# Two embedding features fetched row by row from SyncE and ScalarE beside GpSimd's gathers, their addresses multiplied once

## The chip, the core and the metric

The kernel runs on one core of a Trainium2 chip. A core has a matrix engine (TensorE, PE in the profile, its weight loads PEld), VectorE (DVE), ScalarE (ACT), GpSimd (POOL), a sequencer that mostly issues transfers (SyncE, SP) and 16 DMA engines. The metric is the device time of one execution in microseconds (us); lower is better.

## The reference

A batch of 2048 samples looks up 27 rows of 128 floats, one in each of 27 tables. The 27 vectors, all their 351 pairwise dot products and 16 dense numbers make a row of 3823, which goes through a small network:

```python
e = stack([tbl_f[ids[:, f]] for f in range(27)], axis=1)      # 2048 x 27 x 128
inter = einsum('bfd,bgd->bfg', e, e)[:, triu_i, triu_j]       # 351 pairs
h = concatenate([e.reshape(2048, -1), inter, dense_ctx], 1)   # 3823
h = maximum(h @ W_top1 + b_top1, 0)                           # 512
h = maximum(h @ W_top2 + b_top2, 0)                           # 256
y = h @ W_top3                                                # 1
```

Tables 22 and 23 have 1000 rows each.

## The kernel before

The batch is cut into 16 tiles of 128 samples, numbered 0 to 15. There is no planner: each engine's program is a loop over the tiles with the order written out by hand, and semaphores tie the engines.

**GpSimd** gathers. For every tile it issues one indirect DMA for each feature (L294), which brings 128 rows of one table into one 128-column stretch of `emb`. `emb` has room for one tile only. The features are in seven groups of up to four (0 to 3, ..., 20 to 23, 24 to 26). Before the gathers of group g of tile t, GpSimd waits until TensorE has turned group g of tile t-1 (L286).

**TensorE** turns each feature (a transpose into PSUM, L323, in `turn_group`), after a wait for all gathers of that group. ACT rounds the result to the matmul's format (`split_group`, L609) and DVE takes the rest (L745), so each feature is multiplied three times (L352 to L354). Within a tile the order is: multiply group 0, turn 2 and 3, multiply, turn 4 and 5 (with the columns of the tile before), multiply and finish the columns, turn 6, then 16 units of pairwise products (L377) between multiplies, and towards their end turn groups 0 and 1 of the next tile. The last matmuls of a tile are layer 2 of the tile before (L470). The last tile has an order of its own with finer steps.

**SyncE** loads the first layer's weights in 30 pieces through six stages (L219); a stage is free when DVE has split it (`s_w_lo`). Behind them come seven small loads of ids (L243), the second layer's weights, the dense inputs and constants. After that SyncE fetches feature 23 of seven tiles (3, 5, ..., 15) one row at a time. It loads 32 ids into registers (L261), and for each row works out the offset and issues a DMA of 512 bytes (L266) into `ahead`, which has a place for each of the seven sets. GpSimd leaves those seven gathers out, so it issues 425 in all. In `turn_group` TensorE waits for all 128 rows of a set before it turns group 5 of that tile (L319).

**ACT** issues no DMA before the change. In tile t it rounds groups 1, 2, 3, places the context columns, rounds 4, takes the columns (`take_columns`), rounds 5 and 6, applies the first ReLU, and then copies units of pairwise products (L665) to the tile's end.

Of the kernel before, what the change touches and what calls it, by code (L numbers as in the profile page):

```python
# [5 lines left out]
def dlrm_tower_kernel(nc, dense_ctx, ids, tables, w_top1, b_top1, w_top2, b_top2, w_top3, out):  # L6
    fp32 = mybir.dt.float32
    fp32r = mybir.dt.float32r
    i32 = mybir.dt.int32
    ALU = mybir.AluOpType  # L10
# [46 lines left out]
    AHEAD_TILES = [3, 5, 7, 9, 11, 13, 15]  # L57
    NA = len(AHEAD_TILES)
    LOAD = 32
    HALF = H1 // 2  # L60

    ctx = ExitStack()
    with ctx:
        def sb(name, shape, dt=fp32):
            return ctx.enter_context(nc.sbuf_tensor(name, shape, dt))
# [17 lines left out]
        ahead = sb("ahead", [P, NA, D])  # L83
        idx_ahead = sb("idx_ahead", [NA, P], i32)
# [39 lines left out]
        s_ids_ahead = sem("s_ids_ahead")  # L124
        s_ahead = [sem(f"s_ahead{t}") for t in AHEAD_TILES]
        s_zero = sem("s_zero")
# [31 lines left out]
        def fetched_ahead(t, f):  # L158

            return f == AHEAD and t in AHEAD_TILES  # L160

        def rows_of(t, f):

            if fetched_ahead(t, f):
                return ahead[:, AHEAD_TILES.index(t), :]
            return emb[:, f * D:(f + 1) * D]
# [47 lines left out]
        def _(sp):  # L214
# [7 lines left out]

            sp.dma_start(idx_first[:, :], ids.rearrange("(p t) f -> p t f", t=TILES)[:, 0, :]
                         ).then_inc(s_ids_first, 16)
            sp.wait_ge(s_ids_first, 16)
            for c in range(NF):
                load_weights(c)
                if c == GROUPS[0][-1]:
                    sp.dma_start(idx[:, :, :].rearrange("p t f -> p (t f)"),
                                 ids.rearrange("(p t) f -> p (t f)", t=TILES)).then_inc(s_ids, 16)  # L230
# [10 lines left out]
            with nc.allow_non_contiguous_dma(reason="one id of every row of ids"):  # L241
                for n, t in enumerate(AHEAD_TILES):
                    sp.dma_start(idx_ahead[n:n + 1, :], ids.rearrange(  # L243
                        "(p t) f -> t f p", t=TILES)[t, AHEAD:AHEAD + 1, :]
                        ).then_inc(s_ids_ahead, 16)
# [12 lines left out]
            sp.wait_ge(s_ids_ahead, 16 * NA)  # L258
            for n in range(NA):
                for p in range(0, P, LOAD):  # L260
                    _, picked = nc.values_load_multi_w_load_instructions(  # L261
                        idx_ahead[n:n + 1, p:p + LOAD], engines=[mybir.EngineType.SP],
                        min_val=0, max_val=tables[AHEAD].shape[0] - 1,
                        skip_runtime_bounds_check_because="an id is a row of its table")
                    for i in range(LOAD):
                        sp.dma_start(ahead[p + i:p + i + 1, n, :],  # L266
                                     tables[AHEAD][bass.ds(picked[i], 1), :]
                                     ).then_inc(s_ahead[n], 16)
# [322 lines left out]
        def _(act):  # L591
# [96 lines left out]

            for t in range(TILES - 1):
# [38 lines left out]
        def _(dve):  # L728
# [128 lines left out]

            dve.memset(emb_x[:, :, :, NF:Q].bitcast(fp32), 0.0).then_inc(s_pads, 1)
            dve.memset(cols[:, NCOL - 1:NCOL], 1.0).then_inc(s_ones, 1)
            dve.memset(ones[:, :], 1.0).then_inc(s_ones, 1)  # L860
            for t in range(TILES - 1):
                for g in range(NG):
                    if t == 0:
                        for c in GROUPS[g]:
                            split_weights(c)
# [65 lines left out]
```

## Time and profile before

| what | value |
|---|---|
| median of the runs shown | 563.61 us (563.38 to 564.31) |
| the profiled execution's own time | 564.87 us |
| its span, first to last instruction | 563.1 us |
| PE / POOL / DVE / ACT busy | 93% / 72% / 63% / 42% |
| mean granted TensorE clock | 0.979 of full speed |
| gathers of GpSimd | 425 |
| rows fetched by SyncE | 896 |

Views of the trace are in us from the span's start. An engine's busy time doesn't count instructions that only issue a DMA or work on registers, so SyncE has no busy row at all; its instructions are found by their lines. The chain of work that ended last follows the end back from releaser to releaser.

### The profile page before, as it was taken

The numbers are of one execution on the slowest core, as the hardware profiler recorded it, in microseconds if no ns is written. First come the engines' busy times: TensorE is split into PE (matmuls) and PEld (weight loads), VectorE is DVE, ScalarE is ACT, GpSimd is POOL, SyncE is SP. The second block draws the span as 40 slices with busy tenths as digits, with TensorE's granted clock in tenths as the row PEclk, the third lists the DMA queues.
The fourth block names the chain that finished last, engine by engine and source line by source line (L and its number), as shares of the span: only waits on it lengthen the run. The fifth ranks groups of instructions, "written<-read, shape, count | busy, mean of one in ns | idle before, by whom it ended". The sixth has DMA issues, their size and how long they took to land.

```text
span 563.1 us, 10765 instructions
## 1 busy us (share of the span) xinstructions
PE 523.0 (93%) x2626; PEld 488.8 (87%) x2626; DVE 354.7 (63%) x1176; ACT 234.6 (42%) x721; POOL 408.2 (72%) x443
## 2 busy tenths in 40 slices
PE   0686899999999999999998999999998999989998
PEld 0475799999999999899897999989998999989986
DVE  2654746757584756758474675847567584756855
ACT  2654426262534526252451625345261534516351
POOL 6777777777777777777777777777777777777711
PEclk9896899999999999999998999999999999999999
DMA  7755111211211111111111211121112111111100
GB/s 239 262 192 136 53 54 57 54 54 53 57 54 54 53 59 55 52 54 58 55 54 53 58 53 54 53 58 54 54 52 58 55 52 54 57 53 52 52 15 2
DMA packets 22196, 38.04 MB, mean 68 GB/s; under 512 B 9588, under 2 KB 11508, under 8 KB 22132
## 3 DMA queue, kind: packets, MB, share of 16 engines
q0 software_dynamic: 13600, 27.88, 17.3%
q1 hardware_dynamic: 8532, 9.46, 5.2%
q8 instruction: 21, 0.34, 0.3%
q14 instruction: 43, 0.35, 0.2%
HBM read 37.30 MB, written 0.01 MB: 66 GB/s over the span
## 4 chain that ended last, share of the span: by engine, by line
PE 44%; POOL 38%; issue 13%; DMA 3%; DVE 1%; ACT 1%; SPq 0%; ACTq 0%; POOLq 0%; DVEq 0%
POOL emb L294 38%; PE ps_acc L352 10%; PE ps_acc L353 9%; PE ps_acc L354 9%; PE ps_gram L377 5%; PE ps_t L323 4%; PE ps_gram L470 2%; DMA g_buf<-in_b_top 1%; PE ps_acc L411 1%; PE ps_acc L412 1%; PE ps_acc L417 1%; DMA emb<-in_tbl,idx_first 1%; PE ps_gram L463 1%; ACT g_buf L674 0%; PE ps_gram L406 0%
## 5 line engine op out<-in xcount | busy, mean ns | idle before, releaser
L294 POOL DMA_INDIRECT emb<-in_tbl,idx x398 | 378.0, 950 | 121.5 <-issue 120.2
L352 PE MATMUL ps_acc<-w_hi,emb_x 128*128 128x512 f32 x432 | 197.8, 458 | 2.6 <-DVE emb_x L745 1.7
L353 PE MATMUL ps_acc<-w_lo,emb_x 128*128 128x512 f32 x432 | 175.7, 407 | 0.0
L354 PE MATMUL ps_acc<-w_hi,emb_x 128*128 128x512 f32 x432 | 175.0, 405 | 0.0
L785 DVE COPY g_buf<-ps_gram 32x112 f32<-32x112 f32 x480 | 129.8, 270 | 70.2 <-PE ps_gram L377 63.4
L609 ACT ACTIVATE emb_x<-ps_t 128x512 fp32r<-128x512 f32 (+1 forms) x111 | 63.7, 583 | 227.2 <-PE ps_t L323 208.4
L665 ACT ACTIVATE g_buf<-ps_gram 32x112 f32<-32x112 f32 x480 | 122.3, 255 | 56.2 <-PE ps_gram L377 50.2
L745 DVE TENSOR_TENSOR emb_x<-ps_t,emb_x 128x512 fp32r<-128x512 f32 (+1 forms) x111 | 72.8, 666 | 106.0 <-ACT emb_x L609 103.0
L352 PEld LDWEIGHTS ps_acc<-w_hi,emb_x 128*128 128x128 f32 x432 | 131.1, 304 | 8.7 <-issue 5.8
L353 PEld LDWEIGHTS ps_acc<-w_lo,emb_x 128*128 128x128 f32 x432 | 134.5, 311 | 1.0
L354 PEld LDWEIGHTS ps_acc<-w_hi,emb_x 128*128 128x128 f32 x432 | 132.1, 306 | 1.3
L323 PE MATMUL ps_t<-ident,emb 128*128 128x128 f32 x422 | 61.6, 280 | 28.1 <-DMA emb<-in_tbl,idx_first 19.2
L323 PEld LDWEIGHTS ps_t<-ident,emb 128*128 128x128 f32 x422 | 50.2, 144 | 37.2 <-issue 13.6
L377 PEld LDWEIGHTS ps_gram<-emb_x 128*128 128x128 f32 x480 | 70.0, 191 | 11.5 <-ACT g_buf L665 4.9
L377 PE MATMUL ps_gram<-emb_x 128*128 128x224 f32 x480 | 71.5, 281 | 6.1 <-ACT g_buf L665 4.0
L294 POOL DMA_INDIRECT emb<-in_tbl,idx_first x27 | 26.7, 987 | 9.2 <-issue 7.6
L829 DVE TENSOR_TENSOR cols<-ps_gram,g_buf 128x26 f32<-128x26 f32 (+25 forms) x390 | 31.9, 161 | 0.5
L803 DVE STREAM_TRANSPOSE ps_gram<-g_buf 128x896 f32<-128x896 f32 x15 | 29.0, 1934 | 0.0
L805 DVE STREAM_TRANSPOSE g_buf<-g_buf 128x896 f32<-128x896 f32 x15 | 28.4, 1893 | 0.0
L470 PE MATMUL ps_gram<-w,h_t 128*128 128x256 f32 x112 | 26.5, 380 | 0.0
L470 PEld LDWEIGHTS ps_gram<-w,h_t 128*128 128x128 f32 x112 | 20.2, 190 | 2.2
L731 DVE TENSOR_TENSOR w_lo<-g_buf,w_hi 128x512 fp32r<-128x512 f32 x27 | 17.4, 698 | 5.1 <-ACT w_hi L594 5.1
(78 smaller groups left out, 249.6 us busy)
## 6 DMA issues: line engine op xcount, KB each, us to landing
ahead<-in_tbl SPq DMA_DIRECT2D x896, 0.5 KB
g_buf<-in_W_top SPq DMA_DIRECT2D x29, 256.0 KB, 4.2
emb<-in_tbl,idx POOLq DMA_INDIRECT x398, 2.5
w<-in_W_top SPq DMA_DIRECT2D x1, 512.0 KB, 4.8
emb<-in_tbl,idx_first POOLq DMA_INDIRECT x27, 3.4
g_buf<-in_W_top SPq DMA_DIRECT2D x1, 222.0 KB
idx<-in_ids SPq DMA_DIRECT2D x1, 216.0 KB, 5.5
ctx_rows<-in_dense_ctx SPq DMA_DIRECT2D x4, 32.0 KB, 3.6
```

Of the source, the lines that this page charges most:

```text
L294: pool.indirect_dma_start(out=emb[:, f * D:(f + 1) * D], out_offset=None, in_=tables[f], in_offset=bass.IndirectOffsetOnAxis(ap=rows, axis ...
L323: last = pe.transpose(turned_bank(n, g)[:, :, i], rows_of(t, f), ident[:, :])
L352: pe.matmul(acc, emb_part(0, f), w_hi[:, f, :], start=(f == 0), stop=False)
L353: pe.matmul(acc, emb_part(0, f), w_lo[:, f, :], start=False, stop=False)
L354: last = pe.matmul(acc, emb_part(1, f), w_hi[:, f, :], start=False, stop=False)
L377: last = pe.matmul(ps_gram[:, n % BANKS, i * NJ * XW:(i + 1) * NJ * XW], gram_weights(q), gram_stream(q), start=True, stop=True)
L470: last = pe.matmul(ps_late[:, 0:H2], h1_t[:, k * P:(k + 1) * P], w_2[:, k, :], start=(k == 0), stop=(k == K2 - 1))
L609: act.activation(group_part(0, g), turned_bank(n, g), ACT.Copy).then_inc(s_emb_hi, 1)
L665: last = act.activation(target, source, ACT.Copy)
L745: dve.tensor_tensor(group_part(1, g), turned_bank(n, g), group_part(0, g).bitcast(fp32), ALU.subtract).then_inc(s_emb_lo, 1)
L785: last = dve.tensor_copy(target, source)
L829: last = dve.tensor_tensor(cols[:, c:c + NF - 1 - f], summed[:, f + 1:NF, f], g_turned[:, GE + f, f + 1:NF], ALU.add)
```

## The change

The ids of features 23 and 22 of all tiles are loaded early, by two DMAs that carry them as [tile, sample]; DVE multiplies them once by 512, the bytes of a row (`place_rows`, in tile 0 ahead of the weights of group 2). The table is seen as bytes, so that a loaded register is an offset as it stands. SyncE fetches nine sets of feature 23 (tiles 2, 4, 5, 7, 8, 10, 11, 13, 14) into five places used in turn, and starts inside the weights' loop: three rows behind each weight piece from piece 14 on. ACT fetches feature 22 of tiles 8 and 15, nineteen rows in each of tiles 1 to 14: a load of registers and 11 rows before it rounds group 4, five rows before it rounds group 6, three before it rounds group 2 of the next tile. GpSimd leaves out 11 gathers in place of seven and issues 421.

```diff
-    AHEAD_TILES = [3, 5, 7, 9, 11, 13, 15]
+    AHEAD_TILES = [2, 4, 5, 7, 8, 10, 11, 13, 14]
+    ROW = D * 4
+    ROWS_FROM = 14
+    ROWS_EACH = 3
+    KEPT = 5
+    BESIDE = 22
+    BESIDE_TILES = [8, 15]
+    A_TILE = 19
+    SLOTS = {4: (0, 11), 6: (11, 16), 2: (16, 19)}
...
+            def fetch_rows(first, count):
+                for r in range(first, first + count):
+                    n, p = divmod(r, P)
+                    if p == 0 and n >= KEPT:
+                        sp.wait_ge(s_pe_t, NG * AHEAD_TILES[n - KEPT] + AHEAD // GF + 1)
+                    if p % LOAD == 0:
...
+                    row = table_bytes[bass.ds(loaded[p % LOAD], ROW)]
+                    sp.dma_start(ahead[p:p + 1, n % KEPT, :].bitcast(u8),
+                                 row.rearrange("(o b) -> o b", o=1)).then_inc(s_ahead[n], 16)
...
                 load_weights(c)
+                if c == ROWS_FROM:
+                    sp.wait_ge(s_at_ahead, 1)
+                if c >= ROWS_FROM:
+                    fetch_rows(ROWS_EACH * (c - ROWS_FROM), ROWS_EACH)
+                if c == STAGES:
+                        for n, f in enumerate((AHEAD, BESIDE)):
+                            sp.dma_start(at_ahead[:, n * P:(n + 1) * P], ids.rearrange(
+                                "(p t) f -> t f p", t=TILES)[:, f, :]).then_inc(s_ids_ahead, 16)
...
-                for n, t in enumerate(AHEAD_TILES):
-                    sp.dma_start(idx_ahead[n:n + 1, :], ids.rearrange(
...
-                        sp.dma_start(ahead[p + i:p + i + 1, n, :],
-                                     tables[AHEAD][bass.ds(picked[i], 1), :]
-                                     ).then_inc(s_ahead[n], 16)
+            begun = ROWS_EACH * (NF - ROWS_FROM)
+            fetch_rows(begun, NA * P - begun)
...
+                if BESIDE in GROUPS[g] and t in BESIDE_TILES:
+                    pe.wait_ge(s_beside[BESIDE_TILES.index(t)], 16 * P)
...
+            def fetch_beside(picked, g):
+                n, s_first, loaded = picked
+                for i in range(SLOTS[g][0], min(SLOTS[g][1], len(loaded))):
+                    p = s_first + i
+                    row = beside_bytes[bass.ds(loaded[i], ROW)]
+                    act.dma_start(beside[p:p + 1, n, :].bitcast(u8),
+                                  row.rearrange("(o b) -> o b", o=1)).then_inc(s_beside[n], 16)
...
+                    if t > 0 and g == 4:
+                        picked = load_rows(t)
+                    if t > 0 and g in (4, 6) or t > 1 and g == 2:
+                        fetch_beside(picked, g)
...
+            def place_rows():
+                dve.wait_ge(s_ids_ahead, 32)
+                dve.tensor_scalar(at_ahead[:, :], at_ahead[:, :], ROW, None,
+                                  ALU.mult).then_inc(s_at_ahead, 1)
```

## Rows read from the trace of the kernel before

**Rows 1.** The page: busy time by engine.

```profile
PE 523.0 (93%) x2626; PEld 488.8 (87%) x2626; DVE 354.7 (63%) x1176; ACT 234.6 (42%) x721; POOL 408.2 (72%) x443
```

**Rows 2.** Busy time in stretches of one tile: stretch, length, busy us (instructions) by engine.

```profile
core 0: us, PE busy (x) PEld busy (x) DVE busy (x) ACT busy (x) POOL busy (x), PEclk, DMA share, GB/s
94.93:126.68 31.75, 31.68 (x166) 30.23 (x165) 21.09 (x74) 13.65 (x44) 23.81 (x26) 1.00 0.19 55
190.18:221.93 31.75, 31.68 (x165) 30.20 (x165) 21.05 (x74) 13.65 (x44) 23.83 (x26) 1.00 0.19 55
489.00:520.50 31.50, 29.70 (x157) 28.42 (x156) 19.45 (x69) 11.59 (x38) 23.88 (x26) 1.00 0.19 53
```

**Rows 3.** The chain that ended last, whole span: start, us, what.

```profile
94.93 1.73 PE ps_gram L470 x8
...
221.93 1.73 PE ps_gram L470 x8
235.52 0.95 POOL emb L294
...
498.30 0.94 POOL emb L294
499.55 2.50 DMA emb<-in_tbl,idx
520.54 1.73 PE ps_gram L470 x8
```

**Rows 4.** PE in order of time, round tile 14's group 5: start, us, what, [idle before <- releaser].

```profile
502.09 0.66 PE L323 MATMUL ps_t<-ident,emb 128*128 128x128 f32 x4 [1.80 <-DMA emb<-in_tbl,idx]
502.59 0.49 PE L406 MATMUL ps_gram<-ident,cols 128*128 128x128 f32 x3
```

**Rows 5.** POOL in order of time, its last gathers.

```profile
534.56 0.94 POOL L294 DMA_INDIRECT emb<-in_tbl,idx  x1 [0.30 <-issue]
535.81 0.94 POOL L294 DMA_INDIRECT emb<-in_tbl,idx  x1 [0.30 <-issue]
```

**Rows 6.** SP in order of time, from 19 us.

```profile
19.13 20.55 SPq L219 DMA_DIRECT2D g_buf<-in_W_top  x15
40.00 0.32 SPq L237 DMA_DIRECT2D g_buf<-in_W_top  x1
40.36 0.28 SPq L239 DMA_DIRECT2D g_buf<-in_b_top  x1
40.69 4.97 SPq L243 DMA_DIRECT2D idx_ahead<-in_ids  x7
45.70 0.60 SPq L247 DMA_DIRECT2D w<-in_W_top  x1
...
48.73 0.43 SPq L255 DMA_DIRECT2D w_rows<-in_W_top  x1
```

**Rows 7.** SP's loads of ids and rows: ns min/median/max, first and last start us.

```profile
L261 SPq TENSOR_LOAD <-idx_ahead x28: 2068/2125/2327, 49.3 to 468.4; - x28
L266 SPq FUSED_REGOPS  x896: 37/37/51, 51.4 to 483.2; - x180
L266 SPq MOVE ahead<-in_tbl x896: 29/29/42, 51.5 to 483.3; - x180
L266 SPq DMA_DIRECT2D ahead<-in_tbl x896: 224/225/314, 51.6 to 483.4; - x180
```

**Rows 8.** SP in order of time, 15 rows without a break.

```profile
59.13 5.94 SPq L266 DMA_DIRECT2D ahead<-in_tbl  x15
```

**Rows 9.** DMA issues: KB each, median us to landing.

```profile
idx_ahead<-in_ids SPq DMA_DIRECT2D x7, 0.5 KB, 3.0
idx_first<-in_ids SPq DMA_DIRECT2D x1, 13.5 KB, 1.7
out<-y SPq DMA_DIRECT2D x1, 8.0 KB, 1.4
```

**Rows 10.** SP's waits: us in total, times, longest.

```profile
SPq L219 <- DVE w_lo L731: 26.1, 23, 6.9
```

**Rows 11.** ACT in order of time, tile 3.

```profile
132.11 1.09 ACT L609 ACTIVATE emb_x<-ps_t 128x512 fp32r<-128x512 f32 x2 [3.16 <-PE ps_t L323]
140.23 0.60 ACT L609 ACTIVATE emb_x<-ps_t 128x512 fp32r<-128x512 f32 x1 [6.93 <-PE ps_t L323]
144.94 0.49 ACT L609 ACTIVATE emb_x<-ps_t 128x384 fp32r<-128x384 f32 x1 [2.90 <-PE ps_t L323]
```

**Rows 12.** DVE in order of time, tile 0.

```profile
36.83 0.69 DVE L745 TENSOR_TENSOR emb_x<-ps_t,emb_x 128x512 fp32r<-128x512 f32 x1 [5.99 <-ACT emb_x L609]
```

More of the change, by code:

```diff
@@ L9, in dlrm_tower_kernel @@
     i32 = mybir.dt.int32
+    u8 = mybir.dt.uint8
     ALU = mybir.AluOpType
@@ L56, in dlrm_tower_kernel @@
     AHEAD = 23
-    AHEAD_TILES = [3, 5, 7, 9, 11, 13, 15]
+    AHEAD_TILES = [2, 4, 5, 7, 8, 10, 11, 13, 14]
     NA = len(AHEAD_TILES)
     LOAD = 32
+    ROW = D * 4
[4 more added lines that the diff above has]
+    BESIDE_TILES = [8, 15]
+    NB = len(BESIDE_TILES)
+    A_SET = TILES // 2 - 1
+    A_TILE = 19
+    SLOTS = {4: (0, 11), 6: (11, 16), 2: (16, 19)}
+    assert BESIDE == AHEAD - 1 and A_SET * A_TILE >= P > A_SET * A_TILE - 8
     HALF = H1 // 2
@@ L82, in dlrm_tower_kernel @@
         emb = sb("emb", [P, NF * D])
-        ahead = sb("ahead", [P, NA, D])
-        idx_ahead = sb("idx_ahead", [NA, P], i32)
+        ahead = sb("ahead", [P, KEPT, D])
+        at_ahead = sb("at_ahead", [TILES, 2 * P], i32)
+        beside = sb("beside", [P, NB, D])
         g_buf = sb("g_buf", [P, 2 * Q * XW])
@@ L124, in dlrm_tower_kernel @@
         s_ids_ahead = sem("s_ids_ahead")
+        s_at_ahead = sem("s_at_ahead")
         s_ahead = [sem(f"s_ahead{t}") for t in AHEAD_TILES]
+        s_beside = [sem(f"s_beside{t}") for t in BESIDE_TILES]
         s_zero = sem("s_zero")
@@ L158, in fetched_ahead @@
         def fetched_ahead(t, f):
-            return f == AHEAD and t in AHEAD_TILES
+            return (f == AHEAD and t in AHEAD_TILES) or (f == BESIDE and t in BESIDE_TILES)
         def rows_of(t, f):
-            if fetched_ahead(t, f):
-                return ahead[:, AHEAD_TILES.index(t), :]
+            if f == AHEAD and t in AHEAD_TILES:
+                return ahead[:, AHEAD_TILES.index(t) % KEPT, :]
+            if f == BESIDE and t in BESIDE_TILES:
+                return beside[:, BESIDE_TILES.index(t), :]
             return emb[:, f * D:(f + 1) * D]
@@ L227, in _ @@
                 load_weights(c)
+                if c == ROWS_FROM:
[3 more added lines that the diff above has]
+                if c == STAGES:
+                    with nc.allow_non_contiguous_dma(reason="one id of every row of ids"):
+                        for n, f in enumerate((AHEAD, BESIDE)):
+                            sp.dma_start(at_ahead[:, n * P:(n + 1) * P], ids.rearrange(
+                                "(p t) f -> t f p", t=TILES)[:, f, :]).then_inc(s_ids_ahead, 16)
                 if c == GROUPS[0][-1]:
@@ L687, in take_right_h1, with load_rows @@
                 act.activation(h1_t[:, HALF:H1], ps_t[:, 0, 0:HALF], ACT.Copy).then_inc(s_h1_out, 1)
+            beside_bytes = tables[BESIDE].rearrange("r d -> (r d)").bitcast(u8)
+            def load_rows(t):
+                s_first = (t - 1) % A_SET * A_TILE
+                u = BESIDE_TILES[(t - 1) // A_SET]
+                if t == 1:
+                    act.wait_ge(s_at_ahead, 1)
+                _, loaded = nc.values_load_multi_w_load_instructions(
+                    at_ahead[u:u + 1, P + s_first:P + min(s_first + A_TILE, P)],
+                    engines=[mybir.EngineType.Activation],
+                    min_val=0, max_val=(tables[BESIDE].shape[0] - 1) * ROW,
+                    skip_runtime_bounds_check_because="an id is a row of its table")
+                return (t - 1) // A_SET, s_first, loaded
+            def fetch_beside(picked, g):
[5 more added lines that the diff above has]
+                                  row.rearrange("(o b) -> o b", o=1)).then_inc(s_beside[n], 16)
             for t in range(TILES - 1):
@@ L862, in _ @@
                 for g in range(NG):
+                    if t == 0 and g == 2:
+                        place_rows()
                     if t == 0:
```

18 lines of the change are left out of this document (7 added, 11 removed).

## The prediction

> **What bounds the kernel.** I read the page first: PE is busy 93% and POOL 72%, but POOL's share leaves out the 0.30 us between two gathers, in which it waits for nothing that the profile shows [rows 1, 5]. Its last two gathers start 1.25 us apart, and nothing else runs there, so 425 gathers are 531 us of a queue that never rests. The stretches come next. From 94.93 to 221.93 each tile takes 31.75 us and PE is busy 31.68 of it: there PE is its own bound [rows 2]. The chain says where that ends: until 221.93 it runs through PE, from 235.52 to 499.55 through POOL's gathers alone [rows 3]. At 31.75 us a tile PE would have issued the layer 2 that stands at 520.54 at 221.93 + 9 x 31.75 = 507.7; POOL holds it back by 12.8 us. The last place where it does so is the turning of tile 14's group 5: PE sat idle 1.80 us before 502.09 for a gather [rows 4]. From there the chain stays on PE and its helpers to the end. So the time is the start of that turning plus 563.1 - 502.1 = 61.0 us. I carry out the whole sum for that start.
>
> **GpSimd's part.** By tile 14's group 5 the old kernel had left out six gathers, the new one leaves out ten (nine of feature 23, and feature 22 of tile 8). Four times 1.25 is 5.0 us: by the gathers PE turns group 5 at 497.1. The same four hold at the last gather, which ends at 536.8 [rows 5] and would at 531.8, so nothing later takes over. PE's own pace gives 502.1 - 12.8 = 489.3, plus whatever the start of the kernel loses; it has 7.8 us in hand. If the fetched rows are there, the gain is 5.0.
>
> **SyncE's part: is set nine there at 497.1?** This is new: the last set used to be needed in tile 15 and landed by about 485, some 50 us early; now it is needed in tile 14, at the very turning that sets the end.
>
> A row. Fifteen DMAs span 5.94 us, so a row takes (5.94 - 0.225)/14 = 408 ns [rows 8]. Its three instructions fill 37 + 29 + 225 = 291 ns [rows 7]; the other 117 are gaps, 39 each. FUSED_REGOPS is the multiplication of the id; with offsets in bytes it has nothing to do. It takes its gap along: 408 - 76 = 332 ns. MOVE, which belongs to the DMA with an offset in a register, I leave. Bounds: only 37 ns saved, 371 a row; or MOVE goes as well, 408 - 144 = 264.
>
> A set. Thirty-two rows with their load took (468.4 - 49.3)/27 = 15.52 us [rows 7]. Less 32 x 0.076 that is 13.09, a set 52.4 us. The bounds are 57.3 and 43.7.
>
> The start. SyncE's last issue ahead of the rows ends at 49.2 [rows 6]. Seven small loads go, 40.69 to 45.70: -5.0. Inside the weights' loop it now does 36 rows and two loads of registers (2.17 each) between 19.13 and piece 26, which it issued at 38.15: twelve issues at 0.37, 36 rows at 0.332 and the loads are 20.8 us, to 39.9; piece 26's three rows add 1.0, and with the rest of the pieces the bias goes out some 2.1 late. That much fits only because SyncE waited 26.1 us for DVE in this loop [rows 10]. The two loads of ids are 2048 pieces of 4 bytes each. A load of 128 such pieces cost 0.71 us of issue against 0.28 for a single piece [rows 6], 3.4 ns a piece, 7 us each; if the price is by the DMA and not by the piece, 0.7 each. Of the 1.4 to 14 us one wait for DVE of up to 6.9 takes its share [rows 10], so 0 to 8 are left; I add 1.4, nearer to the lower end, since a DMA of 512 pieces took only 0.60 [rows 6]. The bulk then starts at 49.2 - 5.0 + 2.1 + 1.4 = 47.7.
>
> The end. Nine sets are 471.6; 39 rows and two loads are done, -17.6; 47.7 + 454.0 = 501.7. A small DMA landed 1.4 to 1.7 us after its issue began [rows 9], say 1.3 after its end: 503.0, and PE turns at 503.1. That is 6.0 behind the gathers and 1.0 behind the kernel before. The other sets are each a set's length apart and needed 1.5 tiles (49 us) apart, so their spare time melts from some 27 us at tile 2 to nothing at 14; tile 11's is about 1 us late by this, which PE's hand covers.
>
> **ACT's part.** A load of registers cost SyncE 2.13 us for 32 [rows 7]; for 19 between 1.3 and 2.2. Eleven rows at 332 ns are 3.7: at most 5.9 in an idle time of 6.93. Five rows are 1.7 in 2.90, three 1.0 in 3.16 [rows 11]. All covered, by PE's multiplies. Without cover, ACT rounds group 4 late and behind it takes the columns, for which PE's column matmuls wait. For chance meetings of ACT's issues with SyncE's I add 0.5 us in all to SyncE's way (bounds below). DVE's multiplication is one small operation in tile 0, but it waits for the ids and holds back DVE's weights of group 2; DVE idles 5.99 us before 36.83 in that tile for the gathers behind ACT [rows 12], which swallows up to that much; what is left over, and the weights' 2.1 to 3.5, come out of PE's 7.8.
>
> **The sum.** 503.1 + 0.5 + 61.0 = 564.6 against the span of 563.1, +1.5. The profiled execution's own time was 564.87, the median 563.61; the change on the median gives 565.1.
>
> **The rivals.** *The rows are there in time.* It needs set nine at 497, so a set of at most 51.7 us in place of 52.4, or less loss at the start: 5 ns less in each row are enough. If MOVE goes too (43.7) it is certain. Time 558.6. *One generator for both queues.* If a row's issue holds something that both engines need for all its 225 ns, two streams of rows advance at 450 ns a pair and not at 332; each of ACT's some 240 rows before tile 14 then costs SyncE 0.118 us, 28 us in all, and PE turns at 531: 593. It decides from a hold of 332/2 = 166 ns; below that the two fall into step and nothing is lost. For it speaks that the DMA is 225 of 291 ns of a row; against it that a DMA of 128 pieces took just 0.43 [rows 6], so a single piece should hold little. The trace has no issue from ACT. The Trainium skill (Perfetto Trace Analysis, "DMA Instruction — HWDGE (DVE, Sync)") has this rule: the block that generates descriptors is shared by the two sequencers and locked for one DMA at a time, with the waiting for the lock inside the profiled window. By that rule ACT's and SyncE's DMAs would read longer than 225 ns where they meet. *ACT's rows are dear.* At 0.6 us a row, eleven and a load of 2.0 overflow the slot of 6.93 by 1.7. PE has 7.8 in hand over 13 tiles, 0.6 a tile; with 1.7 it turns group 5 at 489.3 + 13 x 1.7 = 511.4, time 573.4. For it speaks nothing but that the trace has no DMA from ACT. *The multiplications stay.* Nine sets at 62.1 end 87 us later: about 651.
>
> **How the numbers follow.** Main case, set nine the last to arrive within 491 to 511: 0.54, of which 0.32 slower, 0.14 the same, 0.08 faster, since 0.3 us in a set are 2.7 in the time. Rows in time by more, full gain: 0.27. Shared generator 0.12, ACT's rows 0.04, multiplications 0.03, all slower. Faster 0.35, same 0.14, slower 0.51, where the same is within 0.2% (1.1 us), about what a measurement of this kernel can tell from none. The range goes from the full gain, 558.4, to 573, which is a set of 53.3; the main case alone has 559 to 572.
>
> **What would show it.** In the profile after: no FUSED_REGOPS, rows 332 ns apart, set nine's last row issued at about 501.5, PE idle before tile 14's group 5 for `ahead` and not for `emb`, POOL's last gather ending at 531.8. Wrong it is if PE turns that group at 497 for a gather (rows faster), if ACT's DMAs or SyncE's are well over 225 ns (one generator), or if tiles in PE's own stretch are longer than 31.75 (ACT).

## The result, and the profile after

The changed kernel takes 560.81 us (median of 11 runs, 559.98 to 562.93) where the kernel before took 563.98 beside it (11 runs, 562.81 to 564.85): ratio 0.9947, 95% interval 0.9937 to 0.9957. It is faster by 0.5%, 3.2 us; I had forecast 565.1, slower. The profiled execution took 560.3 us with a span of 558.3, 4.8 less than the span before.

The page of the kernel after, busy time by engine, against [rows 1]:

```profile
PE 521.1 (93%) x2626; PEld 488.6 (88%) x2626; DVE 354.7 (64%) x1177; ACT 234.1 (42%) x721; POOL 404.4 (72%) x439
```

The chain that ended last, kernel after, is built as in [rows 3]: PE alone through the early tiles, then gathers, then PE from tile 14 to the end.

```profile
289.26 1.73 PE ps_gram L505 x8
327.39 0.95 POOL emb L327
...
492.29 0.95 POOL emb L327
494.79 2.51 DMA emb<-in_tbl,idx
515.78 1.73 PE ps_gram L505 x8
```

The gather whose transfer is followed from 494.79 had landed at 497.3, and PE turned group 5 of tile 14 then (at 497.34): the same place that set the end before, 4.8 us earlier than 502.1 [rows 4]. 497.3 + 61.0 = 558.3 is the span, to the tenth. PE hardly stood still there, though: its first turnings of that group follow those of group 4 after 0.06 us, where it had idled 1.80 before the change. Its waits for gathers of 0.61, 1.20 and 0.77 us fall on group 5 of tiles 11, 12 and 13 now. The last gather of all, as against [rows 5]:

```profile
530.97 0.94 POOL L327 DMA_INDIRECT emb<-in_tbl,idx  x1 [0.30 <-issue]
```

It ends at 531.91; I had written 531.8, and 497.1 for the turning. So GpSimd's part came out as forecast. What did not is the claim that set nine would arrive after the gathers. SyncE's loads and rows, to be held against [rows 7] (ns min/median/max, then first and last start in us):

```profile
L253 SPq TENSOR_LOAD <-at_ahead x36: 2072/2154/2255, 20.8 to 477.7; - x36
L258 SPq MOVE ahead<-in_tbl x1152: 29/29/29, 22.9 to 490.3; - x192
L258 SPq DMA_DIRECT2D ahead<-in_tbl x1152: 227/228/321, 23.0 to 490.4; - x192
```

The multiplications are gone, and the last row was issued at 490.4, not 501.5. The landing of single rows is not in the trace. With the forecast's 1.3 us behind the issue's end (490.6) it is there at 491.9, 5.4 before PE turns the group. In the runs below in which the rows came last, PE turned 1.4 to 1.8 us behind the start of the last issue, which agrees. SyncE in order of time at the start, kernel after, against [rows 6]:

```profile
7.21 4.54 SPq L273 DMA_DIRECT2D at_ahead<-in_ids  x2
11.79 9.00 SPq L237 DMA_DIRECT2D g_buf<-in_W_top  x8
23.00 1.02 SPq L258 DMA_DIRECT2D ahead<-in_tbl  x3
24.07 0.37 SPq L237 DMA_DIRECT2D g_buf<-in_W_top  x1
...
48.09 0.43 SPq L297 DMA_DIRECT2D w_rows<-in_W_top  x1
48.62 4.47 SPq L258 DMA_DIRECT2D ahead<-in_tbl  x14
```

The two loads of ids hold SyncE for 4.5 us; then three rows go behind each weight piece, 1.4 us from piece to piece. What is left of the 26.1 us of waits for DVE [rows 10] is, in the view of waits:

```profile
SPq L237 <- DVE w_lo L793: 6.0, 10, 1.8
```

The bulk of the rows began at 48.6 (forecast 47.7).

ACT's part of the kernel after: its register loads and its rows by line, and tile 3 in order of time, against [rows 11].

```profile
L732 ACTq TENSOR_LOAD <-at_ahead x14: 1870/4299/4327, 73.0 to 489.6; - x14
L744 ACTq DMA_DIRECT2D beside<-in_tbl x256: 213/214/509, 74.9 to 499.1; - x128
```

```profile
135.99 1.08 ACT L644 ACTIVATE emb_x<-ps_t 128x512 fp32r<-128x512 f32 x2 [3.16 <-PE ps_t L358]
...
140.84 3.75 ACTq L744 DMA_DIRECT2D beside<-in_tbl  x11
144.71 0.60 ACT L644 ACTIVATE emb_x<-ps_t 128x512 fp32r<-128x512 f32 x1 [7.53 <-PE ps_t L358]
```

Most loads of 19 registers take 4.3 us, twice the most I allowed. With 3.75 for eleven rows ACT overruns its slot of 6.93 and rounds group 4 some 0.6 us late (it idled 7.53 before it). PE doesn't feel it: a tile from turning to turning takes 31.74 us with PE busy 31.67 of them, as in [rows 2].

```profile
112.20:143.94 31.74, 31.67 (x167) 30.21 (x166) 20.94 (x73) 13.52 (x44) 23.80 (x27) 1.00 0.20 55
```

### The profile page after: what moved, and what is told of

The parts are those of the page before. It is cut to its first block, busy times and chain, and to the rows that moved or that the text cites. A ratio compares the mean times of both kernels' runs of the same rounds, so it can differ in the third digit from the quotient of the medians.

```text
span 558.3 us, 10910 instructions
## 1 busy us (share of the span) xinstructions
PE 521.1 (93%) x2626; PEld 488.6 (88%) x2626; DVE 354.7 (64%) x1177; ACT 234.1 (42%) x721; POOL 404.4 (72%) x439
## 4 chain that ended last, share of the span: by engine, by line
PE 58%; POOL 27%; issue 9%; DMA 3%; DVE 1%; ACT 1%; SPq 0%; ACTq 0%; POOLq 0%; DVEq 0%
POOL emb L327 27%; PE ps_acc L387 14%; PE ps_acc L388 12%; PE ps_acc L389 11%; PE ps_gram L412 7%; PE ps_t L358 5%; PE ps_gram L505 2%; PE ps_acc L446 1%; DMA g_buf<-in_b_top 1%; PE ps_acc L447 1%; PE ps_acc L452 1%; PE ps_gram L498 1%; DMA emb<-in_tbl,idx_first 1%; PE ps_gram L441 1%; ACT g_buf L709 1%
## 5 line engine op out<-in xcount | busy, mean ns | idle before, releaser
L327 POOL DMA_INDIRECT emb<-in_tbl,idx x394 | 372.9, 946 | 120.2 <-issue 118.7
L358 PE MATMUL ps_t<-ident,emb 128*128 128x128 f32 x418 | 59.9, 278 | 22.9 <-DMA emb<-in_tbl,idx_first 20.1
L412 PE MATMUL ps_gram<-emb_x 128*128 128x224 f32 x480 | 72.7, 283 | 8.4 <-ACT g_buf L700 4.6
L327 POOL DMA_INDIRECT emb<-in_tbl,idx_first x27 | 28.0, 1038 | 9.3 <-issue 7.9
```

Source lines behind the costliest of these rows:

```text
L327: pool.indirect_dma_start(out=emb[:, f * D:(f + 1) * D], out_offset=None, in_=tables[f], in_offset=bass.IndirectOffsetOnAxis(ap=rows, axis ...
L358: last = pe.transpose(turned_bank(n, g)[:, :, i], rows_of(t, f), ident[:, :])
L412: last = pe.matmul(ps_gram[:, n % BANKS, i * NJ * XW:(i + 1) * NJ * XW], gram_weights(q), gram_stream(q), start=True, stop=True)
```

## The experiments

Twelve runs were made, in three groups, each beside its own runs of the kernel before: medians 564.23, 564.98 and 564.5. "g5" is PE's turning of group 5, and "loss" what the gathers took beyond 1.25 us each: the 27 of tile 0 first, then all of them up to the last one that group 5 of tile 14 needs. Times are medians where a kernel was timed; the ratio is estimated from the runs and need not be the quotient of the two medians. With one execution there is no interval.

| kernel | gathers | g5 of tile 1 | g5 of tile 14 | plus 61.0 | span | loss | ratio, 95% interval |
|---|---|---|---|---|---|---|---|
| before | 425 | 76.5 | 502.1 | 563.1 | 563.1 | 1.1, 3.1 | |
| after | 421 | 80.4 | 497.3 | 558.3 | 558.3 | 2.5, 3.1 | 0.9947 (0.9937 to 0.9957) |
| no_head_start | 421 | 81.0 | 509.2 | 570.2 | 571.6 | 4.0, 5.0 | 1.0058 (1.0042 to 1.0075) |
| sync_only | 423 | 80.4 | 500.2 | 561.2 | 561.5 | 3.9, 4.7 | 0.9963 (0.9948 to 0.9977) |
| seven_sets | 425 | 78.0 | 502.5 | 563.5 | 563.4 | 2.3, 3.4 | 1.0022 (1.0013 to 1.0032) |
| pe_own | 409 | 84.6 | 497.8 | 558.8 | 558.7 | 4.0, 5.0 | 0.9904 (0.9880 to 0.9927) |
| ids_late | 421 | 79.9 | 501.5 | 562.5 | 563.7 | 2.8, 3.6 | 0.9983 (0.9959 to 1.0007) |
| ids_twice | 421 | 87.6 | 500.3 | 561.3 | 561.2 | 3.0, 4.2 | 0.9977 (0.9961 to 0.9992) |
| act_load_10 | 421 | 82.5 | 499.7 | 560.7 | 560.7 | 4.8, 5.6 | one execution |
| after_again | 421 | 82.3 | 499.2 | 560.2 | 560.1 | 4.3, 5.0 | 0.9952 (0.9937 to 0.9966) |
| ids_split | 421 | 80.2 | 498.6 | 559.6 | 559.6 | 4.1, 4.5 | 0.9931 (0.9918 to 0.9944) |
| three_sets | 420 | 81.7 | 497.6 | 558.6 | 558.6 | 3.2, 4.5 | 0.9919 (0.9903 to 0.9934) |
| twenty_rows | 421 | 81.4 | 496.8 | 557.8 | 557.9 | 2.3, 2.6 | one execution |
| multiplied_again | 421 | 84.1 | 592.0 | 653.0 | 655.2 | 4.6; later ones wait for PE | one execution |

### no_head_start: SyncE's rows all behind the weights

```diff
-    ROWS_EACH = 3
+    ROWS_EACH = 0
```

> The changed kernel without the rows inside the weights' loop; SyncE fetches all nine sets behind it. The gate theory: the time is the moment at which PE turns group 5 of tile 14, plus 61 us, and that moment is the latest of the gathers (497.3), the landing of set nine, and PE's own pace. Sets of 51.0 us from about 45.5 us end at 504.5 and land at 505.7, so PE turns at 505.8, the span is 566.8 and the time about 568.8, slower than the kernel before by 0.9%. The rival, that PE hides a late set as it hides other waits, expects 560.8, no change against the changed kernel.

Measured: 568.96 us (566.65 to 573.62, 6 runs), for 568.8 expected. The profiled execution was the slowest of the six, 573.62, so its places lie later than those of the median. In it the last row was issued at 507.49, and PE, in order of time, waited 5.40 us and turned tile 14's group 5 1.7 us after it:

```profile
509.15 0.87 PE L358 MATMUL ps_t<-ident,emb 128*128 128x128 f32 x3 [5.40 <-issue]
509.82 0.42 PE L358 MATMUL ps_t<-ident,ahead 128*128 128x128 f32 x1
```

The wait shows no releaser, because the rows are not followed as a transfer of this turning; the last gather that it needed had started at 496.5, so it is `ahead`. The gate of the prediction is real: move set nine past the gathers and the end moves with it. The span is 1.4 more than the gate plus 61.0. From 505.8, two microseconds into this idle, the granted clock was 0.50 for 6.8 us (stretch, length, busy us by engine, granted clock, DMA share, GB/s):

```profile
505.80:512.60 6.80, 3.45 (x12) 3.10 (x13) 1.10 (x3) 1.04 (x3) 5.14 (x6) 0.50 0.21 54
512.60:530.00 17.40, 17.40 (x96) 16.48 (x96) 9.30 (x34) 9.50 (x34) 13.22 (x14) 1.00 0.20 53
```

That is the lower of TensorE's two levels, 1.2 GHz, behind a PE that had idled for 5.4 us; PE was busy 3.45 us at that level; half of that, an estimate, would be 1.7, and the span lost 1.4. It is a price of a missed gate that my sum did not have.

### sync_only: nothing fetched by ScalarE

```diff
-    BESIDE_TILES = [8, 15]
+    BESIDE_TILES = []
...
-                    if t > 0 and g == 4:
-                        picked = load_rows(t)
-                    if t > 0 and g in (4, 6) or t > 1 and g == 2:
-                        fetch_beside(picked, g)
```

> The changed kernel without ACT's two sets of feature 22: GpSimd gathers them again, 423 gathers. Gate theory: PE turns group 5 of tile 14 at 498.5 instead of 497.3, and the last gather ends 2.5 us later, at 534.4, which now is what PE waits for last; span 560 to 560.8, time about 562.2. If one generator served both queues and cost anything, SyncE's rows would come closer together than the 325 ns (mean without loads) that the changed kernel shows; the theory that there is no such cost expects 325 ns again.

Measured: 562.54 us (561.16 to 563.73, 6 runs). SyncE's rows stood 324.8 ns apart on average (starts in the trace, with register loads and distances over 600 ns left out) against 324.9 in the kernel after, and its last row went out at 490.14 against 490.4. ACT's DMAs therefore cost SyncE nothing that can be read. The ratios (0.9963 here, 0.9947 and 0.9952 for the kernel after) put ScalarE's two sets at 0.6 to 0.9 us, but the intervals overlap, so the timed runs don't establish that. The spans differ by 3.2. The turning of tile 14's group 5 came 2.9 later: 1.25 is the gather that ScalarE spares ahead of it, and 1.6 the larger loss of the gathers (4.7 for 3.1). The last 0.3 is a fourth candidate, as expected for this run. PE waited that long for the last gather of all, and the chain ends through it:

```profile
537.62 0.33 PE L374 MATMUL ps_t<-ident,emb 128*128 128x128 f32 x1 [0.33 <-DMA emb<-in_tbl,idx]
```

In the kernel after, PE waits for no gather behind tile 14's group 5, so feature 22 of tile 15 is worth those 0.3 us and feature 22 of tile 8 the 1.25.

### seven_sets: the new row alone

```diff
-    AHEAD_TILES = [2, 4, 5, 7, 8, 10, 11, 13, 14]
...
-    ROWS_EACH = 3
-    KEPT = 5
...
-    BESIDE_TILES = [8, 15]
+    AHEAD_TILES = [3, 5, 7, 9, 11, 13, 15]
...
+    ROWS_EACH = 0
+    KEPT = 7
...
+    BESIDE_TILES = []
...
```

> Only the new row: the tiles of the kernel before (3, 5, ..., 15), seven places, no rows in the weights' loop, no ACT, but ids multiplied once by DVE and loaded early, rows by byte offsets. Theory: rows are 321 ns apart instead of 408, SyncE is done some 70 us earlier, and the time is that of the kernel before (563.1 to 564.7), since its seven sets were early anyway. A rival, that SyncE's register work or the late id loads held the gathers up, expects 1 us or more less, with gathers closer together than 1.2512 us.

Measured: 565.3 us (565.09 to 565.92, 10 runs), 1.1 us above the median of the kernel before beside it and above what was expected. The view of the load's line holds the cleanest measurement of a row:

```profile
L252 SPq TENSOR_LOAD <-at_ahead x28: 2073/2156/2207, 45.5 to 389.7; - x28
```

Thirty-two rows with their load took (389.7 - 45.5)/27 = 12.75 us; before it was 15.52 [rows 7]. The row is 2.77/32 = 87 ns shorter. The last row goes out at 402.0 instead of 483.4, and the time does not fall: rows that arrive earlier buy nothing while 425 gathers set the end. Why it is slower than before is not shown. The two early loads of ids are the suspect: the gathers of tile 0 lost 2.3 us for 1.1. But up to tile 14's group 5 they lost 3.4 for 3.1, and PE's start (g5 of tile 1 at 78.0 for 76.5) does not set the end here. In no_head_start, whose SyncE program is the same up to the bulk, that turning came at 81.0, so one profile each does not price the loads.

### pe_own: how far PE's own pace is

```diff
-            return (f == AHEAD and t in AHEAD_TILES) or (f == BESIDE and t in BESIDE_TILES)
+            return ((f == AHEAD and t in AHEAD_TILES) or (f == BESIDE and t in BESIDE_TILES)
+                    or (f == 0 and 3 <= t <= 14))
```

> The changed kernel with twelve more gathers left out (feature 0 of tiles 3 to 14; the rows of tile 2 stay in their place, so the result leaves them out): what PE takes when nothing fetched holds it back. PE turns group 5 of tile 5 at 207.4 in the changed kernel, at 31.75 us a tile group 5 of tile 14 at 493.2; span 554.2, time 556.2, 4 us below the changed kernel. If something else than gathers and rows has become the bound, the time stays near 560.8.

Measured: 559.4 us (557.24 to 560.51, 4 runs), 3.2 above what was expected; the profiled execution was the slowest of the four. With twelve gathers fewer PE waits for none from tile 3 to 14, and it keeps 31.75 us a tile from 84.6 to 497.8. The level was missed because PE's start is not a constant: in this profile the loads of ids held SyncE 6.7 us, and g5 of tile 1 fell at 84.6, not 80.4. PE's pace is thus at most a few us below the gathers, not 7.8.

### ids_late: only the first set's ids early

The ids of feature 23 of one tile (128) are fetched in the weights' loop, the two loads of 2048 behind the constants, multiplied by DVE in tile 1.

```diff
-                        for n, f in enumerate((AHEAD, BESIDE)):
-                            sp.dma_start(at_ahead[:, n * P:(n + 1) * P], ids.rearrange(
-                                "(p t) f -> t f p", t=TILES)[:, f, :]).then_inc(s_ids_ahead, 16)
+                        t = AHEAD_TILES[0]
+                        sp.dma_start(at_first[:, :], ids.rearrange(
+                            "(p t) f -> t f p", t=TILES)[t, AHEAD:AHEAD + 1, :]).then_inc(s_ids_set, 16)
...
+                for n, f in enumerate((AHEAD, BESIDE)):
+                    sp.dma_start(at_ahead[:, n * P:(n + 1) * P], ids.rearrange(
+                        "(p t) f -> t f p", t=TILES)[:, f, :]).then_inc(s_ids_ahead, 16)
...
```

> The changed kernel, but only the 128 ids of its first set are loaded inside the weights' loop; the two loads of 2048 ids each go out behind the constants, at about 46 us, and DVE multiplies them in tile 1. Theory: the early loads held up the gathers of tile 0 (they lost 2.5 us there in the changed kernel's profile and 2.3 to 4.0 in the four experiments' profiles, against 1.1 in the kernel before) and PE's start; with them gone tile 0 loses about 1.1 to 1.5 us, PE turns group 5 of tile 1 near 77 to 79 instead of 80 to 85, and the time falls by 1 to 2.5 us to 558.3 to 559.8. The rival, that 4096 pieces of 4 bytes cost the gathers the same wherever they stand, expects the loss to move to 46 to 60 us and the time to stay at 560.8.

Measured: 564.98 us (561.29 to 567.37, 12 runs), no gain that can be told from the kernel before. The theory fell twice. The late loads held SyncE from 46.45 to 55.8, 9.3 us, and this pushed the last row to 499.74 and made the rows the gate again; PE in order of time, with the releaser missing as above:

```profile
501.52 0.87 PE L368 MATMUL ps_t<-ident,emb 128*128 128x128 f32 x3 [4.29 <-issue]
502.19 0.42 PE L368 MATMUL ps_t<-ident,ahead 128*128 128x128 f32 x1
```

And g5 of tile 1 came at 79.9, hardly before 80.4: in this profile the start is late without the two large loads in front. The three rows behind each weight piece space the pieces 1.4 us apart in this kernel too.

### ids_twice: the early loads doubled

The two early loads are issued a second time into a spare tile.

```diff
-                        for n, f in enumerate((AHEAD, BESIDE)):
-                            sp.dma_start(at_ahead[:, n * P:(n + 1) * P], ids.rearrange(
+                        for n, f in enumerate((AHEAD, BESIDE, AHEAD, BESIDE)):
+                            sp.dma_start((at_ahead if n < 2 else spare)[:, n % 2 * P:(n % 2 + 1) * P], ids.rearrange(
...
```

> The changed kernel with both early id loads issued a second time, into a place that nobody reads. If the pieces of 4 bytes are what holds up SyncE's weights and the gathers of tile 0, the loss there doubles: SyncE spends 9 us or more on the four issues, tile 0's gathers lose 4 to 7 us against 1.25 each, and the time rises by 2 to 4 us to about 563 to 565. If the loss of tile 0 is chance between executions, the time stays at 560.8.

Measured: 563.56 us (561.88 to 566.13, 12 runs). That lies in the expected 563 to 565, but is only 1.2 above after_again of the same group, and it came another way than by the gathers. The four loads held SyncE 11.6 us, g5 of tile 1 came at 87.6, and from there PE's own pace sets the end: 87.6 + 13 x 31.75 = 500.35, and g5 of tile 14 was at 500.3. This is the cleanest sight of the third candidate of the gate, and it says when a late start costs: in the kernel after it is 80.4 + 412.75 = 493.2, so PE has 4.1 us in hand there. Doubling the loads did not double the loss in tile 0 (3.0).

### act_load_10: ten registers a load

```diff
-    A_TILE = 19
-    SLOTS = {4: (0, 11), 6: (11, 16), 2: (16, 19)}
+    A_TILE = 10
+    A_ROWS = 70
+    SLOTS = {4: (0, 10), 6: (10, 10), 2: (10, 10)}
...
-                    pe.wait_ge(s_beside[BESIDE_TILES.index(t)], 16 * P)
+                    pe.wait_ge(s_beside[BESIDE_TILES.index(t)], 16 * A_ROWS)
...
+            dve.memset(beside[:, :, :], 0.0)
```

> ACT loads 10 registers in a tile instead of 19 and fetches 10 rows, all in the slot before group 4, so that only 70 rows of each set of feature 22 are fetched and the rest of the set stays zero. In the changed kernel ACT's load takes 4.3 us for 19 registers where SyncE's takes 2.1 for 32. A price by the register expects 2.3 us; a fixed price, 4.3 again. SyncE's rows stay 325 ns apart either way.

Measured: 562.7 us in one execution. ACT's loads took 1.17 to 1.19 us and 2.38 to 2.39, the first exactly where the load starts at a multiple of 16 bytes. Neither the 2.3 by the register nor a fixed 4.3 fits.

### after_again: the changed kernel once more

> The changed kernel as it is, for the spread of its times and a second profile. Theory: an execution's time is 61 us behind the moment at which PE turns group 5 of tile 14, and that moment moves with what the gathers of tile 0 and PE's start lose; a median of 560.8 again, and in this profile span = that moment + 61 within 0.3, with set nine landed 4 to 7 us earlier.

Measured: 562.4 us (561.87 to 563.02, 6 runs), 1.6 above what was expected; but the kernel before beside it was higher too (564.98), and the ratio, 0.9952, is that of the first time. Its profiled span was 560.1, 1.8 more than the first, and its g5 of tile 14 came 1.8 later. Most of that is visible on POOL in order of time. First the kernel after, then this run of the same program:

```profile
20.04 1.82 POOL L327 DMA_INDIRECT emb<-in_tbl,idx_first  x1 [0.30 <-issue]
```

```profile
21.57 3.02 POOL L327 DMA_INDIRECT emb<-in_tbl,idx_first  x1 [0.30 <-issue]
```

A gather that lasts 3.02 in place of 0.94, while the weights stream in, is never caught up, since POOL does not rest. Seven of the fourteen traces have such a gather of 2.8 us or more round 20 us, one in each.

### ids_split: feature 22's ids by two loads of 128

```diff
-                        for n, f in enumerate((AHEAD, BESIDE)):
-                            sp.dma_start(at_ahead[:, n * P:(n + 1) * P], ids.rearrange(
-                                "(p t) f -> t f p", t=TILES)[:, f, :]).then_inc(s_ids_ahead, 16)
+                        sp.dma_start(at_ahead[:, :], ids.rearrange(
+                            "(p t) f -> t f p", t=TILES)[:, AHEAD, :]).then_inc(s_ids_ahead, 16)
...
+                for n, t in enumerate(BESIDE_TILES):
+                    sp.dma_start(at_beside[n:n + 1, :], ids.rearrange(
+                        "(p t) f -> t f p", t=TILES)[t, BESIDE:BESIDE + 1, :]).then_inc(s_ids_beside, 16)
```

> The changed kernel with feature 22's ids fetched by two loads of 128 behind the constants instead of the second 2048-id load ahead of the weights, multiplied in tile 1; all else as it is. Theory that the second early load costs the start: SyncE is some 4 us earlier with the weights, PE turns group 5 of tile 1 at 77 to 79 (80.4 with the change), POOL loses less than 2.5 us in tile 0, time 559 to 561. Rival, by which the start of PE and POOL's losses come from SyncE's rows among the weights and not from the ids: group 5 of tile 1 stays at 80, time 561 to 563 as the changed kernel.

Measured: 560.8 us (559.93 to 561.6, 5 runs), in the range; but the signs were those of the rival. g5 of tile 1 stayed at 80.2 and the loss in tile 0 was 4.1. The interval of its ratio overlaps that of the first timing of the kernel after, so a gain over it is not established. SyncE in order of time says why leaving out the second load freed so little. First the kernel after, then this run:

```profile
7.69 4.06 SPq L273 DMA_DIRECT2D at_ahead<-in_ids  x1
11.79 2.50 SPq L237 DMA_DIRECT2D g_buf<-in_W_top  x1
```

```profile
7.57 4.61 SPq L240 DMA_DIRECT2D g_buf<-in_W_top  x1
```

What follows a load of 2048 ids is held, whatever it is: the second load there, a weight piece here. The first weight piece behind the ids was issued by 12.2 instead of 14.3, yet the fourth went out at the same time in both (17.07 and 17.16), since it waits for a free stage.

### three_sets: a third set for ScalarE

This is ids_split with a third set of feature 22 on ACT and every register load starting at a multiple of 16 bytes.

```diff
-    BESIDE_TILES = [8, 15]
+    BESIDE_TILES = [6, 11, 15]
-    A_TILE = 19
-    SLOTS = {4: (0, 11), 6: (11, 16), 2: (16, 19)}
+    A_TILE = 28
+    SLOTS = {4: (0, 12), 6: (12, 20), 2: (20, 28)}
...
```

> The changed kernel with a third feature-22 set fetched row by row by ScalarE (sets of tiles 6, 11 and 15, 28 rows a tile, every register load starting on a multiple of 16 bytes), and with feature 22's ids fetched by three loads of 128 behind the constants and not by a 2048-id load ahead of the weights, multiplied in tile 1. POOL has 420 gathers, not 421. By the gate theory (the end is group 5 of tile 14 plus 61.0 us, and POOL's gathers set it) one gather fewer takes 1.25 us off, and the shorter early load of ids takes off what POOL and PE lose at the start: turning of group 5 of tile 14 at 494.5 to 496.5, time 557 to 559.5. If SyncE's early time does not matter, 559.5 to 561 (1.25 us below the changed kernel). If ScalarE has no room for 28 rows a tile (28 x 0.304 = 8.5 us and a load of about 2.8 us at 99 ns a register), its splits come late and PE's tile grows over 31.75 us: every 0.1 us a tile is 1.4 us at the end, time over 561. If PE's own pace sets the end (it had 4.1 us in hand), the gathers' gain stops there.

Measured: 560.13 us (558.4 to 561.39, 6 runs), ratio 0.9919 against the kernel before. That interval (0.9903 to 0.9934) lies below both of the kernel after (0.9937 and up), so by the ratios this kernel, which computes everything, is faster than the kernel after; the two were not timed in one group. It overlaps that of ids_split (0.9918 to 0.9944) beside it. The time lies above the 557 to 559.5 of the theory and in the 559.5 to 561 that was named for the case that SyncE's early time does not matter. g5 of tile 14 was expected by 496.5 and came at 497.6. PE in order of time shows where it was held last, a tile earlier:

```profile
465.83 0.55 PE L364 MATMUL ps_t<-ident,emb 128*128 128x128 f32 x3 [0.81 <-DMA emb<-in_tbl,idx]
```

and the chain says that this one transfer took 3.42 us from its issue, not 2.5:

```profile
462.37 3.42 DMA emb<-in_tbl,idx
484.29 1.73 PE ps_gram L511 x8
```

From 465.83 PE runs at its own pace, 465.83 + 31.75 = 497.6. The saved gather did not show in this profile, since the others lost 1.4 us more on their way than those of the kernel after (the distances over 1.25 us add up to 4.5 us in place of 3.1). Whether the timed runs show it stays open: against ids_split, from which it differs by that gather and by ScalarE's loads, the median is 0.7 lower, inside the intervals. PE's own pace from tile 1 would give 81.7 + 412.75 = 494.5, so 3 us are left to it.

### twenty_rows: aligned register loads

```diff
-    A_TILE = 19
-    SLOTS = {4: (0, 11), 6: (11, 16), 2: (16, 19)}
+    A_TILE = 20
+    SLOTS = {4: (0, 12), 6: (12, 17), 2: (17, 20)}
```

> The changed kernel with 20 rows a tile on ScalarE in place of 19 (12, 5 and 3 in its three gaps), so that every one of its register loads starts on a multiple of 16 bytes. If a load's price goes by the alignment of its start, all fourteen take 1.9 to 2.1 us (20 registers at 99 ns), where the changed kernel has 4.3 us for most; if by something else (the tile, the data), the 4.3 us ones stay. The time stays at 560 to 563 either way, since ScalarE's late split ends before PE wants it.

Measured: 559.83 us in one execution. The line of ACT's loads:

```profile
L732 ACTq TENSOR_LOAD <-at_ahead x14: 727/1438/1461, 74.0 to 489.3; - x14
```

The 4.3 us are gone, as by alignment, but the price is 1.44 and not 1.9: twenty aligned registers are cheaper than nineteen. The last section says what that gives.

### multiplied_again: the multiplication back in each row

```diff
-                            min_val=0, max_val=(tables[AHEAD].shape[0] - 1) * ROW,
+                            min_val=0, max_val=tables[AHEAD].shape[0] - 1,
...
-                    row = table_bytes[bass.ds(loaded[p % LOAD], ROW)]
-                    sp.dma_start(ahead[p:p + 1, n % KEPT, :].bitcast(u8),
-                                 row.rearrange("(o b) -> o b", o=1)).then_inc(s_ahead[n], 16)
+                    sp.dma_start(ahead[p:p + 1, n % KEPT, :],
+                                 tables[AHEAD][bass.ds(loaded[p % LOAD], 1), :]).then_inc(s_ahead[n], 16)
...
-                dve.tensor_scalar(at_ahead[:, :], at_ahead[:, :], ROW, None,
+                dve.tensor_scalar(at_ahead[:, P:], at_ahead[:, P:], ROW, None,
```

> The changed kernel with SyncE's rows addressed by row number again, so that each row has its multiplying instruction back (feature 23's ids not multiplied ahead); still nine sets on SyncE and two on ScalarE. This is the rival that the multiplications stay. The row costs 408 to 410 ns, a set 62 us, nine sets end some 99 us later than 491.7, at 587 to 591, and the end is set by the landing of set nine: 648 to 653 us. If SyncE's rows were not what gates the ninth set, the time would stay at 561 to 563.

Measured: 657.17 us in one execution; my rival had 651. SyncE's rows by line, and PE in order of time at the gate:

```profile
L257 SPq FUSED_REGOPS  x1152: 37/37/51, 23.2 to 590.5; - x192
...
L257 SPq DMA_DIRECT2D ahead<-in_tbl x1152: 224/225/444, 23.3 to 590.7; - x192
```

```profile
563.69 0.60 PE L357 MATMUL ps_t<-ident,emb 128*128 128x128 f32 x4
592.04 0.87 PE L357 MATMUL ps_t<-ident,emb 128*128 128x128 f32 x3 [27.75 <-issue]
```

One edit to the row, all else alike, moves the last row from 490.4 to 590.7 and the time by 96 us. 592.0 + 61.0 is 653.0; behind the idle PE worked 5.0 us at a clock of 0.50, as in no_head_start, and the span is the other 2.2 us longer. So the multiplication out of the row is what makes nine sets possible at all, and the gathers spared are what pays.

## Why the prediction was wrong

**What held.** The end is the start of tile 14's group 5 plus 61.0: in the eleven traces of the table where PE had not idled over 4 us before that turning it fits the span within 0.3 us, whichever candidate came last. In sync_only the last 0.3 came from the last gather. GpSimd's part is right to 0.2 us (497.3 for 497.1, last gather 531.9 for 531.8). The rival "rows in time" is what happened, with its place and its releaser; its gain of 5.0 us is the profile's, but the medians show 3.2.

**The step that failed is the row, a term that was mis-sized.** "It takes its gap along: 408 - 76 = 332 ns", and from it "Less 32 x 0.076 that is 13.09, a set 52.4 us". By seven_sets a row lost 87 ns, not 76, and 32 rows with their load take 12.75, a set 51.0. In the starts of single instructions the old row is 37 + 36 + 29 + 31 + 225 + 51 = 409 ns (the multiplication, a gap, MOVE, a gap, the DMA, a gap), the new one 29 + 29 + 228 + 36 = 322. I spread the 117 ns of gaps evenly, 39 each. They are not even: the one behind the DMA, ahead of the multiplication, was 51 and is 36 with MOVE behind it. With the multiplication (37) and the gap behind it (36) that makes most of the 87. The even share missed 11 ns. From the bulk's start it is 1113 rows, 8.7 sets, 454.0 by my sum and 442.0 in the trace: 12.0 us, and with 0.9 the other way for the start (48.6 for 47.7) set nine landed at 491.9 and not at 503.0. The prediction said that 5 ns less in a row were enough to turn it over; it then took the value where I should have seen that the case was open, with a chance of 0.54 on one side of a step that the bounds (43.7 to 57.3 a set) straddled. That the rival came true is no merit of the forecast: its direction was wrong, and the term that decided it was off by 12 us. A gap belongs to the pair of instructions on either side of it, and no row of the trace before showed a DMA followed by MOVE.

**SyncE's start.** I added 1.4 us for the loads of ids, between 0 and 8. They held SyncE for 4.5 (4.6 to 6.7 in the other runs with both), and waits for DVE took most of that in. The bulk came 0.9 later than forecast. By seven_sets, with the loads and no rows among the weights, the 1.4 was about right: its rows begin at 45.5, 1.2 later than 49.3 - 5.0. But no_head_start began at 48.3 with the same SyncE program, so this moves by microseconds from one execution to the next, and which term the 0.9 belongs to stays open. Two small sums of the prediction do not come out: 39 rows and two loads are 17.3 by its own terms, not 17.6, and the rival of dear ACT rows gives 572.9, not 573.4. Neither changes a conclusion.

**PE's hand.** I gave PE 7.8 us less what the start loses. The start lost 3.9 (g5 of tile 1 at 80.4 for 76.5), so 3.9 of them were left; by the trace 4.1, between 493.2 and the gathers' 497.3. No cost in the kernel after; in ids_twice and pe_own it was the bound.

**ACT.** "For 19 between 1.3 and 2.2" is wrong: eight of the fourteen loads took 4.3, four 1.9 and two, of 14 ids, 3.2. The rows were cheaper than the 332 ns I took, 304 at the median from start to start. The second error is small against the first: eleven rows saved 0.3 us, a load took 2.1 more than I allowed. Together they are 8.1 us, for at most 5.9. The lateness of 0.6 is covered by PE's multiplies as I had said. The rival of dear rows did not happen.

**One generator for both queues.** Nothing of it shows. Where one of SyncE's DMAs overlaps one of ACT's in time it lasts 230.8 ns on average, where it does not 230.0, and sync_only has the same distance between rows. The Trainium skill (Perfetto Trace Analysis, "DMA Instruction — HWDGE (DVE, Sync)") has the two share a block that is locked for one DMA at a time, the waiting inside the profiled window; here, with one row of 512 bytes in each DMA, the measurement has less than 1 ns for it, and the 28 us of that rival never came.

**Why the medians gained 3.2 and 2.6, and the gathers 5.0.** Between the two profiles the four spared gathers show almost in full, 4.8 us of span. The gathers lost the same in both up to the gate, 3.1 us: 1.1 of it in tile 0 before and 2.5 after, but the later gathers lost 2.0 and 0.6. The two profiled executions were not middle ones, though. The one before took 564.87 us where the median beside the change is 563.98, the one after 560.3 where it is 560.81. These 0.9 and 0.5 are most of the 1.8 us by which 3.2 falls short of 5.0. A further 0.2 is the time outside the span (1.8 us before, 2.0 after), and 0.2 the span at 4.8 and not 5.0. So the median execution of the new kernel lies later than its profile, and that of the old one earlier. Where it loses the time is not shown. In the other profiles of the new start the gathers lost 2.6 to 5.6 us up to the gate. Most of this spread is the one long gather round 20 us. It came in no_head_start (3.03 us) and not in seven_sets (none over 1.5), whose SyncE programs are the same there, and in after_again and not in twenty_rows. So chance between executions has a share in it. All thirteen traces with the new start lose more in tile 0 than the single one of the kernel before, so what SyncE newly does there may have a share too. How much, and what part of it is the ids' or the rows', stays open.

## What to carry to other kernels

When an instruction leaves a short sequence, measure its gap on the side where the neighbours change; when a thousand repeats stand before a gate, 10 ns each decide the sign, so quote both outcomes and not a point between. List every candidate for the gate (here gathers, fetched rows, PE's own pace) with its arrival time: a change pays only until the next candidate, and each of the three was the last one in some kernel here. Work moved into the first microseconds delays PE's start, and once the delay is longer than what PE has in hand, it is paid for at the end in full (ids_twice). And compare medians with medians: a single profile can lie 0.9 us off its kernel's median, which is a quarter of this gain.

## What the runs showed of the hardware

**A load of registers is priced by fours or by ones.** ACT's loads took, by count and by whether their first id lies at a multiple of 16 bytes:

| registers | aligned | not aligned |
|---|---|---|
| 4 | 0.48 us | |
| 8 | 0.73 | |
| 10 | 1.18 | 2.39 |
| 14 | | 3.23 |
| 16 | 1.20 | |
| 19 | 1.88 | 4.30 |
| 20 | 1.44 | |
| 28 | 1.91 | |

About 0.25 us plus 0.235 for each four aligned registers and 0.213 for each single one gives all of these within 0.06: 19 aligned are four fours and three ones, 0.25 + 0.94 + 0.64 = 1.83. SyncE's 32 aligned ones (2.15 us) fit the same line, 0.25 + 8 x 0.235 = 2.13. That it goes by fours is my reading of these sizes. In three_sets two aligned loads, of 12 and of 24 registers, stand directly behind another load; they took 0.79 and 1.50, 0.16 less than this sum, so a load right behind another seems cheaper.

**A row.** One 512-byte DMA with its address in a register costs SyncE 322 ns from start to start (409 with the multiplication) and ACT 304; two engines doing so at once did not slow each other.

**Ids by 4-byte pieces.** Two loads of 2048 pieces issued one behind the other held SyncE between 4.5 and 6.7 us early and 9.3 us behind the constants, while the first was issued in 0.43 to 0.67. What is held is the next DMA: the second load (4.06 in the kernel after), or, with one load alone, a weight piece (4.61 in ids_split, where most such pieces take 0.33 to 0.43). A load's price in front of other work is therefore not that of its own issue.
